# Parts of 32 destinations, each with its own loop over its edge tiles, in a graph kernel's counting stage

## The reference: what is computed

```
trans = einsum('nd,tod->tno', h, W_edge) + b_edge[:, None, :]
msg = trans[etypes, src];  a = segment_sum(msg, dst);  h = gru_cell(a, h, ...)
```

## Time and profile before

| what | value |
|---|---|
| median of 3 runs | 505.75 us (505.05 to 510.2) |
| the profiled execution | 507.11 us |
| its span in the profile | 505.3 us |
| TensorE busy | 428.2 us (85%) |
| VectorE busy | 289.9 us (57%) |
| ScalarE busy | 174.2 us (34%) |
| mean granted TensorE clock | 0.943 |

### The profile page before, as it was taken

How to read it: one execution, slowest core, us unless ns; L and a number is a source line. 1 busy time by engine, 2 the same in 40 slices (tenths; PEclk the granted TensorE clock), 3 DMA queues, 4 the chain that set the end, 5 groups by cost and what they waited for, 6 DMA issues and landing times.

```text
span 505.3 us, 9333 instructions
## 1 busy us (share of the span) xinstructions
PE 428.2 (85%) x3176; PEld 354.5 (70%) x3176; DVE 289.9 (57%) x746; ACT 174.2 (34%) x310; POOL 12.0 (2%) x33
## 2 busy tenths in 40 slices
PE   1387686688887889587979999999999999999995
PEld 0384354476776678565658788887888878988894
DVE  6979888879889873546544544244442344433322
ACT  3620334556657556344322322023220222212111
POOL 2101000000000000100100000000000000000000
PEclk9869977989889889799999999999999999999998
DMA  6000000000000000000000000000000000000000
GB/s 163 21 0 1 1 1 1 1 1 2 1 2 2 2 2 1 0 1 0 3 5 1 0 1 2 1 0 1 1 1 1 0 2 2 0 1 1 1 22 30
DMA packets 5834, 3.56 MB, mean 7 GB/s; under 512 B 495, under 2 KB 5632, under 8 KB 5788
## 3 DMA queue, kind: packets, MB, share of 16 engines
q1 hardware_dynamic: 4516, 2.42, 1.9%
q10 hardware_dynamic: 1272, 0.54, 0.4%
HBM read 2.31 MB, written 0.64 MB: 6 GB/s over the span
## 4 chain that ended last, share of the span: by engine, by line
PE 69%; DVE 15%; issue 6%; ACT 6%; DVEq 3%; DMA 0%; POOL 0%; SPq 0%; ACTq 0%; POOLq 0%
PE small L1428 34%; PE big L1416 7%; PE big L1284 5%; PE small L1301 5%; DVE cell_hot L837 4%; DVE absent L858 3%; DVE absent L854 3%; ACT absent L455 2%; DVEq L837 2%; PE small L1318 1%; PE big L1379 1%; PE big L1381 1%; PE big L1380 1%; PE big L1370 1%; PE big L1371 1%
## 5 line engine op out<-in xcount | busy, mean ns | idle before, releaser
L1428 PE MATMUL small<-nibbles,store 128*128 128x256 fp8e4 (+1 forms) x1600 | 175.2, 270 | 2.9 <-issue 2.9
L1428 PEld LDWEIGHTS small<-nibbles,store 128*128 128x128 f16 x1600 | 156.1, 98 | 24.2 <-issue 8.3
L1284 PE MATMUL big<-cell_hot,store 128*128 128x320 bf16 x264 | 60.9, 359 | 28.2 <-DVE cell_hot L837 20.2
L837 DVE TENSOR_SCALAR cell_hot<-iota,cell_w,fields 128x320 bf16<-128x320 f16 x264 | 75.2, 357 | 13.8 <-issue 6.6
L1284 PEld LDWEIGHTS big<-cell_hot,store 128*128 x264 | 36.1, 144 | 48.1 <-issue 42.1
L1085 DVE TENSOR_SCALAR aS<-small,edge_down 128x256 f32<-128x256 f32 (+1 forms) x20 | 9.6, 478 | 92.6 <-PE small L1428 92.6
L604 ACT CAST store<-digit_words 128x512 f16<-128x512 f32 x40 | 24.5, 618 | 105.4 <-DVE digit_words L998 105.4
L998 DVE TENSOR_TENSOR digit_words<-big,edge_rows 128x512 f32<-128x512 f32 x40 | 27.1, 689 | 27.5 <-PE big L1416 27.5
L1416 PE MATMUL big<-wT,h 128*128 128x512 f32 x80 | 38.1, 597 | 2.3 <-ACT h L600 2.3
L941 DVE SCALAR_TENSOR_TENSOR cell_hot<-rz,cell_hot 128x256 f32<-128x256 f32 (+1 forms) x25 | 10.5, 419 | 35.9 <-ACT cell_hot L575 35.9
L1301 PE MATMUL small<-ident,nibbles 128*128 128x128 f16 x400 | 29.6, 245 | 0.2
(11 more groups left out here) (241 smaller groups left out, 515.7 us busy)
## 6 DMA issues: line engine op xcount, KB each, us to landing
xn<-in_x SPq DMA_DIRECT2D x1, 576.0 KB
out<-xn SPq DMA_DIRECT2D x4, 128.0 KB
store<-in_edge_attr SPq DMA_DIRECT2D x1, 256.0 KB
wn<-in_L_gnn_W_edge SPq DMA_DIRECT2D x1, 256.0 KB, 6.6
wn<-in_L_gnn_Wi ACTq DMA_DIRECT2D x1, 192.0 KB, 4.0
wn<-in_L_gnn_Wh_g ACTq DMA_DIRECT2D x1, 192.0 KB, 6.5
wn<-in_L_gnn_W_ih SPq DMA_DIRECT2D x1, 192.0 KB, 6.4
wn<-in_L_gnn_W_hh SPq DMA_DIRECT2D x1, 192.0 KB, 6.3
```

Of the source, the lines that this page charges most:

```text
L837: last = v.tensor_scalar(half_hot[:, b * GROUP + q], iota[:, b * HALF:(b + 1) * HALF], cell_w[:, half, bass.ds(tile + q, 1)], fields[:, 1, ...
L1284: last = mm(big[:, 2 * half + b, 0:HALF], lane_hot[:, :, bass.ds(tile + q, 1)].rearrange("p l a -> p (l a)"), half_hot[:, b * GROUP + q], ...
L1428: last = mm((psA, psD)[g % 2][:, 0:w], m16[s % 2][:, i, part, t * P:(t + 1) * P], A8[:, t % 2, i, c * CH:c * CH + w, t // 2], start=(i == ...
```

## The change

`GROUP` is 2 and the ring of 8 is kept. The table now has four fields to a window: first tile and number of groups for each of the two parts, so that each part's number of tiles is its own, rounded up to 2. `edge_tiles` unpacks the four. In `one_hots` and `window` each part has a hardware loop of its own. A round handles 2 tiles, and the place in the ring is no longer fixed in the code but computed from the running number of tiles (`ring_slot`). On TensorE each part's bank is waited for, opened and closed by itself, and `K.window` and `K.evac` count parts instead of windows. On ScalarE `evac` converts each bank in a copy of its own.

```diff
--- before.py
+++ after.py
@@ -36,16 +36,16 @@
 ET = -(-E // P)
 EFULL = E // P
 EREST = E - EFULL * P
-GROUP = 4
-RING = 2 * GROUP
+GROUP = 2
+RING = 8
 SLOW = 5
 LANE_PART = 20
 WIN = 64
 SUB = WIN // 2
 NW = NP // WIN
 NS = NP // SUB
-ETP = -(-ET // GROUP) * GROUP
-assert ETP % LANE_PART == 0 and ETP % SLOW == 0
+ETP = -(-ET // LANE_PART) * LANE_PART
+assert ETP % GROUP == 0 and ETP % SLOW == 0
 SLOTS = NW * ETP
 CELLS = NT * WIN
 HALF = CELLS // 2
@@ -137,9 +137,10 @@
         above = sb("above", [P, 2, NS], F32)
         ranks = sb("ranks", [P, 2, 2, NS], F32)
         best80 = sb("best80", [2 * NS, 1], F32)
-        rg_i = sb("rg_i", [1, 2, NW], I32)
+        rg_i = sb("rg_i", [1, 2, NW, 2], I32)
         rg_f = sb("rg_f", [1, 2, NW, 2], F32)
-        rg_n = sb("rg_n", [1, 3, NW], F32)
+        rg_n = sb("rg_n", [1, 2, NW, 2], F32)
+        rg_w = sb("rg_w", [1, 3, NW], I32)
         table = sb("table", [1, NW], I32)
         fields = sb("fields", [P, 3, ETP], F32)
 
@@ -270,14 +271,21 @@
 
 
         def edge_tiles(eng, j, ahead):
-            word = eng.value_load(table[0:1, j:j + 1], min_val=0, max_val=65536 * (ETP + 1))
-            first, second, tiles = eng.snap(word & 255), eng.snap((word >> 8) & 255), eng.snap(word >> 16)
-            return (first, second, tiles, ahead), eng.snap(ahead + 2 * tiles)
+            word = eng.value_load(table[0:1, j:j + 1], min_val=0, max_val=(1 << 24) * (ETP // GROUP + 1))
+            firsts = eng.snap(word & 255), eng.snap((word >> 8) & 255)
+            tiles = eng.snap(((word >> 16) & 255) * GROUP), eng.snap((word >> 24) * GROUP)
+            middle = eng.snap(ahead + tiles[0])
+            return ((firsts[0], tiles[0], ahead), (firsts[1], tiles[1], middle)), eng.snap(middle + tiles[1])
 
 
         def sub_tile(first, k):
             return nc.s_assert_within(first + k, 0, ETP - GROUP, skip_runtime_bounds_check_because=
                                       "first is a tile of edges, and the groups from it on end within ETP")
+
+
+        def ring_slot(before):
+            return nc.s_assert_within(before & (RING - 1), 0, RING - GROUP, skip_runtime_bounds_check_because=
+                                      "the tiles before a group are a multiple of GROUP")
 
 
         def slow_tile(s, J, t):
@@ -440,13 +448,13 @@
                 return last
 
             def evac(J, half):
-                act.wait_ge(K.window, 2 * J + half + 1)
                 if J > 0:
                     act.wait_ge(K.digits, J)
-                o = packed.rearrange("p (i d) -> p i d", i=NT)[:, :, half * WIN:(half + 1) * WIN]
-                a.copy(o.rearrange("p i (b d) -> p b i d", b=2),
-                       big[:, 2 * half:2 * half + 2, 0:HALF].rearrange("p b (i d) -> p b i d", d=SUB)
-                       ).then_inc(K.evac, 1)
+                o = packed.rearrange("p (i d) -> p i d", i=NT)
+                for b in range(2 * half, 2 * half + 2):
+                    act.wait_ge(K.window, 4 * J + b + 1)
+                    a.copy(o[:, :, b * SUB:(b + 1) * SUB], big[:, b, 0:HALF].rearrange("p (i d) -> p i d", d=SUB)
+                           ).then_inc(K.evac, 1)
 
             def absences(n):
                 act.wait_ge(K.countT, n + 1)
@@ -788,18 +796,19 @@
             dve.wait_ge(S0.best_T, 1)
             dve.wait_ge(C.const, 5)
             up, down = (psB[0:1, q * NS:(q + 1) * NS].rearrange("p (w b) -> p w b", b=2) for q in range(2))
-            begin, tiles_of, room = rg_f[:, 0], rg_n[:, 0], rg_n[:, 1]
+            begin, groups_of, room = rg_f[:, 0], rg_n[:, 0], rg_n[:, 1]
             link(v.tensor_scalar(rg_f[:, 1], down, -1.0, 2.0 * P, ALU.mult, ALU.add))
             link(v.tensor_tensor(begin, rg_f[:, 1], up, ALU.min))
             link(v.tensor_tensor(rg_f[:, 1], up, begin, ALU.subtract))
-            link(v.tensor_tensor(rg_n[:, 2], rg_f[:, 1, :, 0], rg_f[:, 1, :, 1], ALU.max))
-            link(v.tensor_scalar(rg_i[:, 0], rg_n[:, 2], GROUP - 1.0, None, ALU.add))
-            link(v.tensor_scalar(rg_i[:, 1], rg_i[:, 0], 2, None, ALU.logical_shift_right))
-            link(v.tensor_scalar(tiles_of, rg_i[:, 1], 1.0, float(GROUP), ALU.max, ALU.mult))
-            link(v.tensor_scalar(room, tiles_of, -1.0, float(ETP), ALU.mult, ALU.add))
-            link(v.tensor_tensor(begin, begin, room.unsqueeze(2).to_broadcast([1, NW, 2]), ALU.min))
-            link(v.scalar_tensor_tensor(rg_n[:, 2], begin[:, :, 1], 256.0, begin[:, :, 0], ALU.mult, ALU.add))
-            v.scalar_tensor_tensor(table[:], tiles_of, 65536.0, rg_n[:, 2], ALU.mult, ALU.add).then_inc(S0.table, 1)
+            link(v.tensor_scalar(rg_i[:, 0], rg_f[:, 1], GROUP - 1.0, None, ALU.add))
+            link(v.tensor_scalar(rg_i[:, 1], rg_i[:, 0], 1, None, ALU.logical_shift_right))
+            link(v.tensor_scalar(groups_of, rg_i[:, 1], 1.0, None, ALU.max))
+            v.scalar_tensor_tensor(rg_w[:, 0], groups_of[:, :, 1], 256.0, groups_of[:, :, 0], ALU.mult, ALU.add)
+            link(v.tensor_scalar(room, groups_of, -float(GROUP), float(ETP), ALU.mult, ALU.add))
+            v.tensor_scalar(rg_w[:, 2], rg_w[:, 0], 16, None, ALU.logical_shift_left)
+            link(v.tensor_tensor(begin, begin, room, ALU.min))
+            link(v.scalar_tensor_tensor(rg_w[:, 1], begin[:, :, 1], 256.0, begin[:, :, 0], ALU.mult, ALU.add))
+            v.tensor_tensor(table[:], rg_w[:, 2], rg_w[:, 1], ALU.bitwise_or).then_inc(S0.table, 1)
             dve.wait_ge(S0.fields, 2)
             window_cells(0, 0)
             window_cells(1, 1)
@@ -824,24 +833,23 @@
 
 
             def one_hots(j, half, tiles_of):
-                first, second, tiles, ahead = tiles_of
                 dve.wait_ge(K.cellw, j + 1)
-                dve.sem_inc(K.taken, 1)
-                with dve.Fori(0, tiles, GROUP) as k:
-                    before = dve.snap(ahead + 2 * k)
-                    for b, begin in enumerate((first, second)):
-                        tile = sub_tile(begin, k)
-                        for u in range(0, GROUP, 2):
-                            dve.wait_ge(K.slot, before + b * GROUP + u + 2)
-                            for q in (u, u + 1):
-                                last = v.tensor_scalar(half_hot[:, b * GROUP + q], iota[:, b * HALF:(b + 1) * HALF],
-                                                       cell_w[:, half, bass.ds(tile + q, 1)],
-                                                       fields[:, 1, bass.ds(tile + q, 1)],
-                                                       ALU.is_equal, ALU.mult)
-                            last.then_inc(K.pair, 2)
+                for b, (first, tiles, ahead) in enumerate(tiles_of):
+                    dve.sem_inc(K.taken, 1)
+                    with dve.Fori(0, tiles, GROUP) as k:
+                        before = dve.snap(ahead + k)
+                        tile, slot = sub_tile(first, k), ring_slot(before)
+                        dve.wait_ge(K.slot, before + GROUP)
+                        for q in range(GROUP):
+                            last = v.tensor_scalar(
+                                half_hot[:, bass.ds(slot + q, 1)].rearrange("p a c -> p (a c)"),
+                                iota[:, b * HALF:(b + 1) * HALF],
+                                cell_w[:, half, bass.ds(tile + q, 1)], fields[:, 1, bass.ds(tile + q, 1)],
+                                ALU.is_equal, ALU.mult)
+                        last.then_inc(K.pair, GROUP)
 
             def read_digits(n):
-                dve.wait_ge(K.evac, 2 * n + 2)
+                dve.wait_ge(K.evac, 4 * n + 4)
                 pk = packed.rearrange("p (i d) -> p i d", i=NT)
                 v.tensor_scalar(nibbles[:, 0, :, n * P:(n + 1) * P], pk, LOW_NIBBLES, None, ALU.bitwise_and)
                 v.tensor_scalar(nibbles[:, 1, :, n * P:(n + 1) * P], pk, 4, LOW_NIBBLES,
@@ -1268,27 +1276,23 @@
 
 
             def window(j, half, tiles_of):
-                if later(j, 2):
-                    pe.wait_ge(K.evac, j - 1)
-                for b in range(2):
+                for b, (first, tiles, ahead) in enumerate(tiles_of):
+                    if later(j, 2):
+                        pe.wait_ge(K.evac, 2 * j + b - 3)
                     mm(big[:, 2 * half + b, 0:2], zero16[:, 0:P], zero16[:, 0:2], start=True, stop=False,
                        skip_group_check=True)
-                first, second, tiles, ahead = tiles_of
-                with pe.Fori(0, tiles, GROUP) as k:
-                    before = pe.snap(ahead + 2 * k)
-                    for b, begin in enumerate((first, second)):
-                        tile = sub_tile(begin, k)
-                        for u in range(0, GROUP, 2):
-                            pe.wait_ge(K.pair, before + b * GROUP + u + 2)
-                            for q in (u, u + 1):
-                                last = mm(big[:, 2 * half + b, 0:HALF],
-                                          lane_hot[:, :, bass.ds(tile + q, 1)].rearrange("p l a -> p (l a)"),
```

(20 more changed lines are left out.)

## The result

The changed kernel takes **846.17 us** (median of 4 runs, 844.09 to 846.86), the kernel before 505.96 us (505.05 to 510.2): the ratio is 1.669, interval 1.6607 to 1.6774. I forecast 540 us in a range of 515 to 562. The direction was right and the size was off by ten: +340 us instead of +33.

The account below looks back on a forecast made before the run. The counting stage was taken as bound by VectorE and a circle of waits: +37.6 (VectorE's line) + 3.6 (window words) - 8.6 (wait before `row_max`) = +32.6 us on 507.1 gave 539.7, forecast 540 us, range 515 to 562.

Parts of the forecast that it names:

- What a round costs: Counting loop: a round of 2 tiles takes 1.10 us, bounds 1.0 to 1.4, mostly sequencer steps and two one-hots.
- the wait (0.045): In each round of 2: the semaphore wait costs 0.045 us.
- TensorE's side of the circle doesn't take its place: Counting turns: once VectorE's 8.6 us wait before `row_max` is used up, no wait on TensorE replaces it.
- The price of a small round: VectorE's counting loop: rounds of 2 follow at 1.10 us; 89 of them make 97.9 us.
- the ring's place: In each round: a mask and an address per one-hot, 2 to 3 single register instructions, 0.11 us.
- The second part: Each window's second loop: its entry costs a semaphore step, a MOVE and a fused instruction more, 0.25 us.
- The window words (+3.6): `next_range` on VectorE: unpacking four fields is exposed in nine turns at 0.4 us, +3.6 us (nothing to 7).
- 1 (register work hides): Rival for the counting loop: the sequencer runs ahead, 0.273 us a tile stays, giving 495 us; 5%.
- 2: Rival: register work partly hidden, rounds of 0.75 to 0.95 us; 0.85 gives 518 us; 15%.
- 4: Rival: break-even, rounds of 0.72 us or fewer on the path, within 1% of now; 5%.
- Rival 3: TensorE becomes the slower counting loop, 1.3 to 1.4 us a round, giving 553 to 565 us; 15%.
- The branch by itself: If the branch were all a round adds, 76 would cost 8 us by the page; register work is larger.

Follow-up runs that it names:

- e1: The changed kernel with TensorE's running number of tiles put into a register once for each window: 569.08 us.
- e3: The changed kernel with the running number put into a register once only, between windows 9 and 10: 700.03 us.
- e6: e1 with VectorE's one wait on `K.pair` outside the loops replaced by a wait on `K.window` with a constant number: 847.37 us.
- e12: The kernel before, running number in a register, rounds of 8, with the ring place computed at run time for every two one-hots: 533.13 us.
- e8: The kernel before, running number in a register, with each part's bank waited for, closed and converted by itself: 502.93 us.
- e5: The changed kernel with one more TensorE wait on `K.pair` for the running number, ahead of each window: 584.03 us.

## Why the prediction was wrong, step by step

**The step that failed** is "What a round costs", in the words "the wait (0.045)", and with them the bounds of 1.0 to 1.4 us. I took `before + GROUP` for one single instruction on a number that lies in a register, so that a round costs the same in window 0 and in window 19. For VectorE this held, because of a use elsewhere. On TensorE (line 1287) the wait's pairs grow from none to 19 or 20 a round, and a round of two products from 1.40 to about 7 us. e1, e3 and e6 show it: 277 of the 340 us. No bound of mine could hold it, since both were drawn from rows of VectorE's line and of TensorE's window 1. The one line that had the sign, 1282, with its 83 fused instructions of 204 ns at the median from 60.7 us on, more than two for each of 33 rounds, had no part in it.

**"TensorE's side of the circle doesn't take its place"** failed with it: VectorE waits 37.7 us before `row_max`. In e1, where the sum is gone, the step holds: 0.7 us.

**The price of a small round** was low, within its bounds. VectorE's rounds in the changed kernel are 1.256 us apart in window 0 against 1.10, 0.64 us of one-hots and 0.62 of pause:

```profile
43.85 0.64 DVE L844 TENSOR_SCALAR cell_hot<-iota,cell_w,fields 128x320 f16 x2 [0.62 <-issue]
45.10 0.64 DVE L844 TENSOR_SCALAR cell_hot<-iota,cell_w,fields 128x320 f16 x2 [0.62 <-issue]
```

Line 844 has four fused and two single register instructions a round (436 and 218 in 109 rounds), where I had put two fused ones and three to five single ones: the ring's place took fused instructions (93 ns) for single ones (45 ns). With the counts of the trace my sum comes to 1.17 us, and 0.08 us stay unaccounted for. By its size the place was nearly right: 0.11 us and two or three steps of 0.038 are about 0.2, and e12 has 0.23 us for two one-hots (30.1/132). The mechanism was right: register work isn't hidden in a short round, and is in a round of 8 at fixed places.

**The second part** has a term that my sum left at nothing: not the entry alone, each of its rounds is longer. In e1, in a turn, a round inside the first loop has 0.65 and 0.63 us of idle time before it, one inside the second 0.82 and 1.06 (the starts at 165.74 and 173.90). That is where line 842 has its pair. The entry itself, the first round of the second loop against the next one, is 0.20 and 0.38 us more (164.27 and 172.21), near the 0.25 of my sum:

```profile
162.61 0.64 DVE L844 TENSOR_SCALAR cell_hot<-iota,cell_w,fields 128x320 f16 x2 [0.65 <-issue]
164.27 0.65 DVE L844 TENSOR_SCALAR cell_hot<-iota,cell_w,fields 128x320 f16 x2 [1.02 <-PE big L1289]
165.74 0.65 DVE L844 TENSOR_SCALAR cell_hot<-iota,cell_w,fields 128x320 f16 x2 [0.82 <-issue]
...
167.25 1.49 DVE L881 SCALAR_TENSOR_TENSOR exp_a<-exp_a,count 128x1280 f32<-128x1280 f32 x1
168.87 0.63 DVE L844 TENSOR_SCALAR cell_hot<-iota,cell_w,fields 128x320 f16 x2
170.14 0.64 DVE L844 TENSOR_SCALAR cell_hot<-iota,cell_w,fields 128x320 f16 x2 [0.63 <-issue]
172.21 0.64 DVE L844 TENSOR_SCALAR cell_hot<-iota,cell_w,fields 128x320 f16 x2 [1.44 <-issue]
173.90 0.64 DVE L844 TENSOR_SCALAR cell_hot<-iota,cell_w,fields 128x320 f16 x2 [1.06 <-issue]
```

At 0.17 us (0.82 - 0.65) the 50 rounds of second parts come to an estimated 8.5 us. No run keeps the second loops and takes this pair away.

**The window words (+3.6)** cost nothing there: `weigh` ends at 168.74 and the one-hots start at 168.87, as closely as before (141.83 and 141.98).

VectorE's own line accounts for e1: its one-hots and the idle time before them, by its own issue and by TensorE, are 70.5 + 60.2 + 20.6 = 151.3 us against 75.2 + 6.6 + 2.4 = 84.2 before, +67; less the 8.1 us of the wait before `row_max` this gives +59, and measured are +63. My sum had 115.5 us for the line, and a steady turn of e1 takes 18.1 us from first one-hots to first one-hots (161.30 to 179.44) where I had about 16.

**The rivals.** 1 (register work hides), 2 and 4 are refuted: even e1 is 12% slower. Rival 3, TensorE the slower loop at 1.3 to 1.4 us a round, names the right engine and in window 0 the right pace (1.40), but has nothing that grows with the windows; it gives 553 to 565. That e1 stands near this with 569 is a coincidence: there TensorE's round is down to 1.21 us, and VectorE waits 20.6 us for TensorE and 60.2 for its own issue. No rival of mine could reach 846.

**What held.** 218 products in 109 rounds; nothing behind the counting stage; no cost of the banks by part (e8). The branch by itself is not the price of a round either: VectorE's is 56 ns at the median of a pause of 0.62 us. On TensorE it took 76 ns at the median before and has a median of 212 ns in the changed kernel. There 69 of the 109 are followed by another round, before it was 13 of 33, so the longer ones are probably those that go round; no run tests it. The Trainium skill ("Advanced Engine Details and Errata", "Control Flow Timing") gives about 108 ns; the trace has less and more than that.

```profile
L1284 PEldq COMPARE_BRANCH  x109: 76/212/353, 35.5 to 522.4; - x109
```

**What stays open.** The computed place was priced on both engines together: TensorE's products go from 346 to 397 ns in e12, the granted clock of the span from 0.948 to 0.903, and how much of the 30 us is VectorE's sequencer and how much TensorE's wasn't separated. VectorE's one-hots and the idle time put down to its own issue grow from 81.8 to 100.5 us there, its waits for TensorE from 0.8 to 7.2. Why a use outside the loop keeps the number is read from what the programs do, not from how they are compiled.

## What to carry to other kernels

A running number that a loop uses, built up over an unrolled sequence, must lie in a register of its own at the end of each step (`alloc_register`, `reg_mov`, `snap`); else each round may add up its whole history. A use of the number outside the loops holds it too (e5), and taking such a use away loses it (e6). Before pricing a round, read the register instructions of every line in it on every engine, by count and by first and last start: more of them than rounds, or growing pauses put down to "issue", is the sign. Fewer products are worth their 0.27 us each only if what they bring with them (more rounds, computed addresses) costs less.

## What the runs showed of the hardware

- A pair of a single and a fused register instruction (32 and 192 ns on TensorE, 40 and 241 on VectorE) costs 0.32 to 0.34 us of the program when nothing covers it; 832 of them are 277 of the 340 us by which this one grew (with the fused instructions of line 1284 in e1's share).
- The granted clock is lower where TensorE pauses (0.56 between 400 and 500 us), and that costs again: the 400 transposing products of the count turns take 39.4 us in the changed kernel and in e1 against 29.6. In e1 this is hidden, as the wait before `row_max` of 0.7 us shows.
- A computed destination takes from VectorE's loop the gapless pace that it has at fixed places: 3.38 us for 8 one-hots against 2.3.
